# A state-space layer with a routed expert layer behind it: another order on GpSimd, earlier spare rows, more slots

## The reference

```python
# first half, a state-space layer with heads
h = rmsnorm(layernorm(x)); proj = h @ w_in_proj           # z, x, B, C, dt
xc = silu(conv4(x) + conv_b); dt = softplus(dt @ w_dt + b_dt)
# chunked scan: M = exp(differences of the cumulated log decays), G = C B^T
y = (M * G) @ xc + exp(lcs) * (C @ state);  state = decay * state + ...
y = (y + xc * D) * silu(z);  y = rmsnorm(y)
x = x + layernorm(layernorm(x) + y @ w_out_proj)
# second half, eight experts, each token goes to two of them
p = softmax(layernorm(x) @ Wg); top two, their shares sum to 1
out = sum over the two: share * (relu(layernorm(x) @ W1[e] + b1[e]) @ W2[e] + b2[e])
x = x + layernorm(out)
```

## Time and profile before

| | us |
|---|---|
| median of 3 runs | 1099.35 (1098.7 to 1101.97) |
| the profiled execution | 1096.12 |
| its span, first to last instruction | 1093.6 |
| TensorE busy | 802.2 |
| VectorE busy | 727.3 |
| GpSimd busy | 678.7 |
| ScalarE busy | 655.6 |

### The profile page before, as it was taken

How to read it: one execution, slowest core, us unless ns; L and a number is a source line. 1 busy time by engine, 2 the same in 40 slices (tenths; PEclk the granted TensorE clock), 3 DMA queues, 4 the chain that set the end, 5 groups by cost and what they waited for, 6 DMA issues and landing times.

```text
span 1093.6 us, 24134 instructions
## 1 busy us (share of the span) xinstructions
PE 802.2 (73%) x7431; PEld 651.8 (60%) x7431; DVE 727.3 (67%) x2183; ACT 655.6 (60%) x1449; POOL 678.7 (62%) x1019
## 2 busy tenths in 40 slices
PE   4799999889898898898898987420676766667000
PEld 2587787667677676677677776420566655556000
DVE  6578888887977987888878875461344443444475
ACT  4687878667676776676676674110455654554375
POOL 7156655767767867767677666764255555556444
PEclk9899999999999999999999998655789899998555
DMA  6000000000000000000000004002222232222475
GB/s 188 3 4 2 5 5 3 15 16 12 19 14 17 17 17 16 15 18 17 14 17 13 18 13 119 31 32 64 74 77 76 74 81 74 80 74 65 115 199 147
DMA packets 60014, 50.83 MB, mean 46 GB/s; under 512 B 10438, under 2 KB 53729, under 8 KB 59888
## 3 DMA queue, kind: packets, MB, share of 16 engines
q1 hardware_dynamic: 51248, 32.23, 11.2%
q0 software_dynamic: 8640, 17.06, 4.9%
HBM read 25.76 MB, written 23.37 MB: 45 GB/s over the span
## 4 chain that ended last, share of the span: by engine, by line
PE 35%; POOL 17%; issue 15%; ACT 11%; DVE 9%; DMA 6%; another core or an unknown queue 4%; DVEq 2%; SPq 1%; ACTq 0%; POOLq 0%
POOL expert_rows L1277 5%; PE bank L851 4%; PE bank L648 3%; DMA moe_pair<-expert_results 3%; PE bank L923 3%; POOL y L1010 3%; PE bank L1879 3%; PE bank L650 2%; PE bank L649 2%; POOL zt L1003 2%; PE bank L906 2%; PE bank L835 2%; PE bank L638 2%; PE bank L837 2%
## 5 line engine op out<-in xcount | busy, mean ns | idle before, releaser
L1904 POOL DMA_INDIRECT expert_results<-moe_y,moe_dest x142 | 140.2, 987 | 123.3 <-DVE moe_y L1897 81.5
L1277 POOL DMA_INDIRECT expert_rows<-xall,row_index x128 | 133.6, 1044 | 44.4 <-issue 39.8
L648 PE MATMUL bank<-thi,whi 128*128 128x512 f32 x224 | 107.5, 480 | 38.7 <-ACT xtok L943 32.6
L935 ACT ACTIVATE m<-bank 128x512 f32<-128x512 f32 x128 | 70.2, 593 | 89.9 <-PE bank L837 89.4
L1817 PE MATMUL bank<-ident,moe_h 128*128 128x128 f32 x142 | 31.5, 307 | 89.5 <-ACT moe_h L1805 85.9
L1019 DVE TENSOR_TENSOR mg<-bank,m 128x512 f32<-128x512 f32 x128 | 82.3, 685 | 17.2 <-PE bank L851 16.0
L1010 POOL TENSOR_TENSOR y<-y,zt 128x256 f32<-128x256 f32 x64 | 56.3, 879 | 58.4 <-issue 34.0
L1879 PE MATMUL bank<-moe_w,moe_hid 128*128 x568 | 88.1, 303 | 4.0 <-ACT moe_hid L1865 2.6
L650 PE MATMUL bank<-thi,wlo 128*128 128x512 f32 x224 | 90.9, 406 | 0.0
L649 PE MATMUL bank<-tlo,whi 128*128 128x512 f32 x224 | 90.6, 405 | 0.0
L1824 ACT ACTIVATE moe_t_hi<-bank 128x256 fp32r<-128x256 f32 x71 | 27.2, 383 | 94.8 <-remote 85.4
(11 more groups left out here) (231 smaller groups left out, 2567.6 us busy)
## 6 DMA issues: line engine op xcount, KB each, us to landing
moe_block_in<-expert_rows SPq DMA_DIRECT2D x71, 132.0 KB
moe_pair<-expert_results SPq DMA_DIRECT2D x16, 512.0 KB, 4.2
out_dram<-moe_outb SPq DMA_DIRECT2D x16, 256.0 KB, 2.5
expert_results<-moe_y,moe_dest POOLq DMA_INDIRECT x142
parts<-csplit SPq DMA_DIRECT2D x128, 4.0 KB
rows<-csplit SPq DMA_DIRECT2D x128, 4.0 KB
expert_rows<-xall,row_index POOLq DMA_INDIRECT x128
expert_rows<-spare_row SPq DMA_DIRECT2D x9, 132.0 KB, 2.1
```

The costliest lines, as they stand in the source:

```text
L648: PE.matmul(bank[:], whi[:, w], thi[:], start=True, stop=False)
L935: SE.activation(m[:, hf * HH:(hf + 1) * HH, :], banks[2 + hf][:].rearrange("p (h l) -> p h l", l=P), ACT.Exp).then_inc(m_ready.sem, 1)
L1277: PL.indirect_dma_start(buckets, bass.IndirectOffsetOnAxis(row_index[:, k, t:t + 1], 0), xall[:, t, :], None).then_inc(scattered, 16)
L1904: PL.indirect_dma_start(back_d, bass.IndirectOffsetOnAxis(dest[:, b % BACK, n:n + 1], 0), yout[:, b % BACK, n, :], None, bounds_check=2 * ...
```

## The change

- In `pool_body` the gate stands directly behind the tile's products and the history, ahead of the powers and the scatters of that tile.
- The scatters of group 12 stand one tile's each in tiles 2 and 3 of the last group, and the other two tiles' behind the loop; the scatters of group 13 follow in one piece.
- The expert stage has eight result slots (`BACK`) where there were four, and six block slots (`IN`) where there were four.
- SP waits only for the third step of the table before it writes the spare rows, and for the rest of the table and all scatters after them.
- The last stage has six pair buffers where there were three, laid into the two buffers of the first weights, which nothing reads by then; five loads are issued at once, and the others five groups ahead of the output.

```diff
--- before.py
+++ after.py
@@ -91,7 +91,7 @@
             for step, when in zip(steps, ((g, 1), (g, 2), (g, 2), (g, 3), (g, 3), (g + 1, 0), (g + 1, 0), (g + 1, 0))):
                 put(step, q, when)
             for i in range(TG):
-                put("scatter", (q, i), (g + 1, 2 + i // 2))
+                put("scatter", (q, i), (g + 1, 2 + i) if i < 2 else end)
         elif q == GROUPS - 3:
             for step, when in zip(steps, ((g, 1), (g, 2), (g, 1), (g, 2), (g, 3), (g, 3), end, end)):
                 put(step, q, when)
@@ -1406,11 +1406,11 @@
     def pool_body(pl, t, i, g, f, par, tp, fr, dyn, norm, moe, seq, end_of_batch, begin, fu):
         pool_tile(pl, t, i, g, par, tp, begin)
         has_post = not (isinstance(g, int) and g == 0)
-        if i == 0:
-            if f is not None:
-                pool_history(pl, f, fu, fu == 0)
-            if has_post:
-                pool_post1(pl, g - 1, 1 - par)
+        if i == 0 and f is not None:
+            pool_history(pl, f, fu, fu == 0)
+        pool_gate(pl, t, i, g, par, tp)
+        if i == 0 and has_post:
+            pool_post1(pl, g - 1, 1 - par)
         if i == 1 and norm:
             pool_norm(pl, g + 2, dyn)
         if i == 3 and has_post:
@@ -1419,7 +1419,6 @@
             pool_route_norm(pl, q)
         for q, k in plan("scatter", g, i):
             pool_scatter(pl, q, k)
-        pool_gate(pl, t, i, g, par, tp)
 
     def over_sequences(eng, body, moe):
         for u in range(GB):
@@ -1543,10 +1542,10 @@
         over_sequences(pl, pool_body, moe)
         pool_squares(pl, T_LAST, T_LAST % 2)
         pool_post1(pl, G_LAST, 1)
-        for i in range(2):
-            pool_scatter(pl, GROUPS - 3, i)
+        for i in range(2, TG):
+            pool_scatter(pl, GROUPS - 4, i)
         pool_post2(pl, G_LAST)
-        for i in range(2, TG):
+        for i in range(TG):
             pool_scatter(pl, GROUPS - 3, i)
         for q in (GROUPS - 2, GROUPS - 1):
             pool_route_norm(pl, q)
@@ -1629,7 +1628,7 @@
     PE, DVE, SE, PL = nc.tensor, nc.vector, nc.scalar, nc.gpsimd
     I32 = mybir.dt.int32
     NT = BLK // P
-    IN, BACK = 4, 4
+    IN, BACK, PAIRS = 6, 8, 6
 
     ident, neghalf, ones = att.ident, att.neghalf, att.ones
     turn_banks, up_banks, down_banks, small_bank = banks[0:2], banks[2:6], banks[6:8], banks[1]
@@ -1666,7 +1665,9 @@
     yout = sb("y", [P, BACK, NT, D])
 
     share = sb("share", [P, 4, TILES])
-    pair = sb("pair", [P, 3, TG, 2, D])
+    held = [w1[:].rearrange("p e k h -> p (e k h)").bitcast(F32)[:, n * 2 * GT:(n + 1) * 2 * GT] for n in range(4)]
+    held += [w1f[:].rearrange("p e h -> p (e h)")[:, n * 2 * GT:(n + 1) * 2 * GT] for n in range(2)]
+    pair = [v.rearrange("p (t k d) -> p t k d", t=TG, k=2) for v in held]
     acc = sb("acc", [P, 2, TG, D])
     st6 = sb("st6", [P, TG, 6])
     mv = sb("mv", [P, TG, 2])
@@ -1695,7 +1696,7 @@
     dest_ready = sig("destinations_ready")
     y_ready = sig("y_ready")
     returned = [nc.alloc_semaphore(f"moe_rows_returned{n}") for n in range(BACK)]
-    pair_loaded = [nc.alloc_semaphore(f"moe_pair_loaded{n}") for n in range(3)]
+    pair_loaded = [nc.alloc_semaphore(f"moe_pair_loaded{n}") for n in range(PAIRS)]
     scaled = sig("first_scaled", TG)
     mixed = sig("mixed", TG)
     stats = sig("out_stats", 2 * TG)
@@ -1910,19 +1911,19 @@
         return 16 * NT * len(range(slot, NBLK, BACK))
 
     def act_scale(act, g):
-        act.wait_ge(pair_loaded[g % 3], 16 * (g // 3 + 1))
+        act.wait_ge(pair_loaded[g % PAIRS], 16 * (g // PAIRS + 1))
         if g >= 2:
             act.wait_ge(normed.sem, normed.of(g - 2))
         for i in range(TG):
             t = g * TG + i
-            SE.activation(acc[:, g % 2, i, :], pair[:, g % 3, i, 0, :], ACT.Copy, scale=share[:, 2, t:t + 1]
+            SE.activation(acc[:, g % 2, i, :], pair[g % PAIRS][:, i, 0, :], ACT.Copy, scale=share[:, 2, t:t + 1]
                           ).then_inc(scaled.sem, 1)
 
     def dve_mix(dve, g):
         for i in range(TG):
             t = g * TG + i
             dve.wait_ge(scaled.sem, scaled.of(g, i + 1))
-            DVE.scalar_tensor_tensor(out=acc[:, g % 2, i, :], in0=pair[:, g % 3, i, 1, :], scalar=share[:, 3, t:t + 1],
+            DVE.scalar_tensor_tensor(out=acc[:, g % 2, i, :], in0=pair[g % PAIRS][:, i, 1, :], scalar=share[:, 3, t:t + 1],
                                      in1=acc[:, g % 2, i, :], op0=ALU.mult, op1=ALU.add).then_inc(mixed.sem, 1)
         if g >= 1:
             dve.wait_ge(coef.sem, coef.of(g - 1))
@@ -1966,14 +1967,15 @@
         sp.dma_start(w2[:, :, 1, :], w2_d.rearrange("e (n p) d -> n p e d", p=P)[1]).then_inc(loaded, 16)
         sp.dma_start(b2[:], b2_d.rearrange("(o e) d -> o e d", o=1).to_broadcast([P, NE, D])).then_inc(loaded, 16)
 
-        sp.wait_ge(att.scattered, att.scattered_all)
-        sp.wait_ge(table.sem, TABLED)
+        sp.wait_ge(table.sem, 3)
         for e in range(NE):
             at = sp.value_load(pad_at[0:1, e:e + 1], min_val=0, max_val=NE * BUCKET)
             sp.dma_start(rows_d[bass.ds(at, BLK), :].rearrange("(n p) c -> p n c", p=P), att.dummy[:]
                          ).then_inc(pads_done, 16)
         sp.wait_ge(att.spare_rows, 16)
         sp.wait_ge(pads_done, 16 * NE)
+        sp.wait_ge(table.sem, TABLED)
+        sp.wait_ge(att.scattered, att.scattered_all)
         for b in range(NBLK):
             if b >= IN:
                 sp.wait_ge(hn_ready.sem, hn_ready.of(b - IN))
@@ -1986,15 +1988,16 @@
             sp.wait_ge(returned[n], returns(n))
         got = back_d.rearrange("(t p k) d -> p t k d", p=P, k=2)
         ov = out.rearrange("b (n p) d -> p (b n) d", p=P)
-        for g in range(GROUPS + 2):
+        for g in range(PAIRS - 1):
+            sp.dma_start(pair[g], got[:, g * TG:(g + 1) * TG]).then_inc(pair_loaded[g], 16)
+        for o in range(GROUPS):
+            g = o + PAIRS - 1
             if g < GROUPS:
-                if g >= 3:
-                    sp.wait_ge(mixed.sem, mixed.of(g - 3))
-                sp.dma_start(pair[:, g % 3], got[:, g * TG:(g + 1) * TG]).then_inc(pair_loaded[g % 3], 16)
-            if g >= 2:
-                o = g - 2
-                sp.wait_ge(out_ready.sem, out_ready.of(o))
-                sp.dma_start(ov[:, o * TG:(o + 1) * TG, :], outb[:, o % 3]).then_inc(stored[o % 3], 16)
+                if g >= PAIRS:
+                    sp.wait_ge(mixed.sem, mixed.of(g - PAIRS))
+                sp.dma_start(pair[g % PAIRS], got[:, g * TG:(g + 1) * TG]).then_inc(pair_loaded[g % PAIRS], 16)
+            sp.wait_ge(out_ready.sem, out_ready.of(o))
+            sp.dma_start(ov[:, o * TG:(o + 1) * TG, :], outb[:, o % 3]).then_inc(stored[o % 3], 16)
         for n in range(3):
             sp.wait_ge(stored[n], 16 * len(range(n, GROUPS, 3)))
```

## The result

| | median of the runs | profiled execution | its span | clock |
|---|---|---|---|---|
| before | 1099.1 us | 1096.12 us | 1093.6 us | 0.895 |
| after | 1182.6 us (1177.2 to 1189.6) | 1177.19 us | 1175.0 us | 0.854 |

The changed kernel is slower: 1.075 times the time before, 95% interval 1.071 to 1.079. I had forecast 1062 us. It ended on the side of rival (c), with a second loss that no rival had foreseen.

A forecast was written before the change was run, and what follows sets the result against it. It took attention as bound by TensorE, with GpSimd adding time once scatters begin, and the expert stage as gapped on every engine. +31 + 6 - 11.8 - 55 - 7.3 = -37.1 gave 1059, with 3.2 for the median 1062 us, range 1020 to 1094.

The forecast's parts named there:

- rival (c): Attention: waits grow because half-clock restarts delay y and the gate in a loop; 8 us a group, 1119 us; chance 0.08.
- Part 1: Attention, gate ahead of powers and scatters: TensorE waits for the sum of squares, some at half clock; +31 us (9 to 62).
- The three waits are 6.2 a group, on top of the 37.3: Attention: waits in tiles 3, 0 and 1 added to TensorE's own time give 43.5 us a group, a loss of 0.8.
- 2.1 to 2.3 is less than the 2.70 that did it: Attention: waits shorter than the one that halved the clock, so rather less than the middle taken: +2.8 us a group.
- Part 2: Routing tail, group 15: the gate first adds GpSimd idle time, partly offset by waits that fall away; +6 us (3 to 9).
- Part 3: Spare rows written early, beside the scatter builds, so their time goes away whole: -11.8 us, 0 as the other bound.
- Part 5: Last stage, loads five ahead: groups follow by 3.58 us where they took 4.14; -7.3 us (0 to -8).
- Part 4: Expert stage, more slots: GpSimd's descriptor building becomes the next bound at 2.57 us a block; -55 us, -25 as other bound.
- Rival (a): Attention: the gate is free or wins because TensorE is late elsewhere; 0 to -59 us, total 1016; chance 0.13.
- Rival (b): Expert stage: VectorE's weight copies hold GpSimd up, 3.0 us a block, 30 us given back, total 1092; chance 0.13.

The follow-up runs named there:

- e5: The changed kernel with needless TensorE products before the output projection in tiles 1 and 2 of groups 3 to 14: 1149.4 us on chip 9.
- e1: The changed kernel with the gate and the plan of the last scatters put back: 1015.3 us on chip 3, 1015.1 on chip 2.
- e2: The kernel before with only the gate moved ahead and its scatter plan: 1178.1 us on chip 3, 1.098 of before.
- e6: e1 with only the group's two first power steps moved behind the gate in tile 0: 1059.6 us on chip 9, 1005.2 on chip 2.

## Why the prediction was wrong, point by point

**What bounds the kernel.** Attention by TensorE and GpSimd: right. "The expert stage: 71 blocks, every engine with gaps" was where I should have asked which engine each gap waits for. ScalarE's 85.4 us of waits for "remote" were the largest wait of that stage.

**Part 1: the mechanism right, the size off.** The chain from y to the sum of squares was well worked out, and TensorE waits where I said, three times a group. The step that failed is "The three waits are 6.2 a group, on top of the 37.3", with the clock at 2.0. Per group TensorE's idle time is 92.7 / 11 = 8.4, of it 7.8 at L892, not 6.2, and the slow clock stretches its products by about 4, not 2 (34.8 / 11 = 3.2 more than before, which itself had 0.9: 20.5 us at half clock, halved, over 11). 37.5 + 8.4 + 4.1 = 50.0. I had taken the times at which y was ready and TensorE asked from the trace before, as if they stood still, and had the clock fall after fewer than half of the waits, for 3 us and a little. It fell twenty times for 28 waits, and for 6.0 us in the mean. And each wait delays the products that y needs, hence y, hence the gate: the 4.03 of GpSimd above. Groups 0 to 3 cost 9.5 (5.4 and 4.1 by L994), which I had put at nothing. Group 3, without a scatter, took 42.7 us for 37.3: one wait of 1.8 us at L892 and 6.8 us at half clock. That also answers "2.1 to 2.3 is less than the 2.70 that did it": 1.8 did it too.

**Rival (c)** had this loop, its place and its order of size (8 us a group, 1119 in all). I gave it 0.08, because the slow stretch of the earlier trace rows "ended by itself within a tile". It does so after as well. What the argument missed is that it comes back in the next tile. e5 shows by experiment what two thirds of the half clock are worth, 2.5 us a group.

**Part 2** is +6.8 for +6 (3 to 9) by L994, and +7.4 between e1 and e2. The mark matters: by L1053, which moved, it would be +2.5, and by VectorE's sum of group 15's first tile (L1034) +9.1. The sum fits; its terms, 6.0 and 4 of idle time against 2 to 7 that fall away, were not parted by any run. **Part 3** is -12.7 for -11.8, with the cover that was named. **Part 5** is -7.6 for -7.3, and the pace of 3.58 is met to the hundredth.

**Part 4: the step "GpSimd's own descriptor building is the next bound".** On chips 2 and 3 it holds: 182.7 us from first to last return for the 183 forecast, GpSimd without pauses. The gain there is 221 - 185 = 36 and not 55, because the stage before was shorter there too. On the chip of the first traces the next bound was another: TensorE's completions. These bursts were there before. With four slots they shared the time with the wait for returns; with that wait gone, one burst follows the other by the time of two blocks (7.1 to 7.4 us) or three (10.2). The stage even takes 10 us more (3 on chip 9), in part perhaps since TensorE there runs at a mean clock of 0.86 after and 0.94 before; that was only read, not tested.

**Rival (a)** fell as a whole: no tile let the gate go free. e6 shows the part of it that was real, the 1.5 us of powers. **Rival (b)** is settled: where no bursts occur, the stage takes 2.57 us a block and not 3.0, so VectorE's copies don't hold GpSimd up. The Trainium skill's rule (SBUF — State Buffer, "SBUF: two separate sides"), by which VectorE in a 2-port mode would block GpSimd's descriptor writes, shows here only faintly: the 142 builds of e1 take 0.991 us in the mean. Of the 74 that overlap VectorE's copy of the weights (0.46 us) six take over 1.05, up to 1.21; of the 68 that don't, none is above 1.0. That is 1 us in the whole stage, where the rival asked for 30. No run shows whether that copy is in a 2-port mode. The prediction's "builds in it show no stretched length" was not quite so: the trace before has four over 1.05, up to 1.21.

**The sum.** On a chip without bursts the right sum would be +98 (attention) and +7 (tail), both from e2 and e1, then -12, -36 and -7: +50, and 1122.4 - 1069.4 = 53 is measured. On the first chip it is +81: there the slots gained nothing.

## What stays open

What holds TensorE's completions on the first chip and chip 9. It goes with the chip, or with the hour at which it was met, and not with the kernel: every kernel profiled on chip 9 has it, the old one included, and none on chips 2, 3 and 5. Chip 9 was met in one set of runs only, so the two are not parted; and the first chip may itself have been chip 9. It strikes SP's queue in the same moments. Whether run-time values, SP's issuing or GpSimd's descriptors bring it on was never tested where it occurs; nor is it known whether something outside this program brings it on. That the holding ends with a load being issued is a coincidence in time, seen in the trace, and no proof of cause: on chip 9 half of the changed kernel's bursts lie near no load.

## What to carry to other kernels

Before an instruction is moved ahead of others on a shared engine, write down what those others will now stand in front of. If it is something that TensorE waits for, add the time at half clock behind each wait, and then go round the loop once more with the new times. Where a wait is removed, list the other waits of that stretch by size, on all engines, before calling the next engine the bound. And take a gain of under 5% for real only after it has been seen on more than one chip.

## What the runs showed of the hardware

- The same program differs by chip, or by the set of runs: before takes 1069 to 1073 us on chips 2, 3 and 5, 1095 on chip 9 and 1099 on the first. Some 18 us of that lie in the expert stage (221 and 239 us); attention agrees within 2% (the changed kernel: 50.0, 50.4 and 50.9 a group in three sets).
- On the slow ones, completions of TensorE come in bursts, 3.1 us late in the one shown, with SP's queue in steps of 0.72 us. TensorE's modelled rows don't show it; the engines that wait for it do, as "remote" or as an end long after the product.
- Waits of 4.25 and 2.89 us each brought 6.8 us at 1.2 GHz, in the first case from inside the wait on, and TensorE was busy through nearly all of what lay behind the wait; a wait of 1.8 us brought 6.8 us too. Needless products in two waits of each group (twenty instructions, 2.39 us, in the one shown) took the time at half clock from 123 to 41 us and made the kernel 2.5% faster.
- Between a wait and the slow clock there is no fixed bond: 13 waits of 2.6 us in the mean were followed by six slow stretches, 28 of 3.0 us by twenty.
- GpSimd's building of descriptors was stretched by at most 0.23 us, in 6 of 74 cases, by a VectorE copy of 128 x 512 at the same time.
